# Self attention in a two-layer decoder: GpSimd rounds the fourth key tile's powers, ScalarE raises that tile once

## What is computed

```python
q, k, v = split_heads(x @ w_q), split_heads(x @ w_k), split_heads(x @ w_v)
attn = jax.nn.softmax(jnp.einsum('bnqd,bnkd->bnqk', q, k) * HEAD_DIM ** -0.5, axis=-1)
o = jnp.einsum('bnqk,bnkd->bnqd', attn, v)
y = merge_heads(o) @ w_proj + b_proj + x
y = (y - mean(y)) * rsqrt(var(y) + EPS) * ln_gamma + ln_beta
```

## Time and profile before

| | us |
|---|---|
| median of 3 runs | 2188.49 (2183.98 to 2189.59) |
| the profiled execution | 2170.81 |
| its span on the core | 2169.0 |
| self attention in it | about 52 to 1053 |
| sequence 3 in it | 430.15 to 554.74 |
| granted TensorE clock, mean | 0.887 of 2.4 GHz |

### The profile page before, as it was taken

How to read it: one execution, slowest core, us unless ns; L and a number is a source line. 1 busy time by engine, 2 the same in 40 slices (tenths; PEclk the granted TensorE clock), 3 DMA queues, 4 the chain that set the end, 5 groups by cost and what they waited for, 6 DMA issues and landing times. The chain is left out here.

```text
span 2169.0 us, 43206 instructions
## 1 busy us (share of the span) xinstructions
PE 1670.8 (77%) x13315; PEld 1065.8 (49%) x13332; DVE 1538.7 (71%) x3296; ACT 1447.3 (67%) x2314; POOL 761.0 (35%) x733
## 2 busy tenths in 40 slices
PE   3889999999999999999479887222444579987677
PEld 1455555555555555555357765122222356665323
DVE  6877777787777777777443666574788478776765
ACT  2889989889898988989334665653556334442845
POOL 0444545555454545546200000455000355553000
PEclk9999999999999999999867988655667689998799
DMA  6223222223222222222142220172010411331002
GB/s 196 54 53 67 55 65 57 67 56 67 55 65 57 66 54 55 67 55 67 32 157 78 79 75 5 60 251 88 30 58 20 135 37 26 34 39 20 1 10 69
DMA packets 173818, 139.96 MB, mean 65 GB/s; under 512 B 83794, under 2 KB 155399, under 8 KB 173366
## 3 DMA queue, kind: packets, MB, share of 16 engines
q1 hardware_dynamic: 166710, 122.78, 21.2%
q0 software_dynamic: 6912, 14.71, 3.5%
HBM read 61.92 MB, written 20.97 MB: 38 GB/s over the span
## 5 line engine op out<-in xcount | busy, mean ns | idle before, releaser
L580 ACT ACTIVATE a_p_hi<-ps,a_probs_up,a_s_scale 128x512 f16<-128x512 f32 x512 | 397.8, 777 | 70.0 <-ACTq L578 69.2
L581 ACT ACTIVATE a_probs<-ps,a_probs_up,a_s_scale 128x512 f32<-128x512 f32 x512 | 397.6, 777 | 0.0
L695 DVE TENSOR_REDUCE a_top<-ps 128x2 f32<-128x1024 f32 x256 | 313.2, 1223 | 118.6 <-DVEq L694 118.5
L927 POOL TENSOR_TENSOR a_p_lo<-a_probs,a_p_hi 128x1024 f16<-128x1024 f32 x128 | 277.4, 2167 | 244.3 <-POOLq L926 201.8
L915 POOL TENSOR_TENSOR a_ops<-a_ident_down,a_top 64x256 f16<-64x256 f32 x256 | 159.8, 624 | 288.1 <-POOLq L910 279.6
L704 DVE TENSOR_TENSOR a_p_lo<-a_probs,a_p_hi 128x1024 f16<-128x1024 f32 x128 | 183.8, 1436 | 39.2 <-DVEq L703 39.2
L441 PE MATMUL ps<-a_ops 128*128 128x512 f16 x512 | 195.1, 381 | 14.6 <-PEq L439 14.3
L460 PE MATMUL ps<-a_v_hi,a_p_hi 128*128 128x65 f16 x2048 | 202.1, 196 | 4.4 <-PEq L455 4.2
L463 PE MATMUL ps<-a_v_lo,a_p_hi 128*128 128x64 f16 x2048 | 202.1, 194 | 0.0
L464 PE MATMUL ps<-a_v_hi,a_p_lo 128*128 128x65 f16 x2048 | 202.1, 195 | 0.0
L460 PEld LDWEIGHTS ps<-a_v_hi,a_p_hi 128*128 128x128 f16 x2048 | 189.1, 98 | 25.1 <-issue 14.2
(11 more groups left out here) (497 smaller groups left out, 3702.9 us busy)
## 6 DMA issues: line engine op xcount, KB each, us to landing
a_ops<-a_qk SPq DMA_DIRECT2D x384, 128.0 KB, 2.3
f_w<-in_L_ffn_W_dram SPq DMA_DIRECT2D x16, 1024.0 KB, 7.4
a_qd<-a_qk SPq DMA_DIRECT2D x128, 64.0 KB, 2.2
g_stage<-in_L_attn_gp_w_dram SPq DMA_DIRECT2D x8, 1024.0 KB, 6.0
X<-in_x_dram SPq DMA_DIRECT2D x8, 512.0 KB, 9.6
expert_in<-f_outT SPq DMA_DIRECT2D x8, 512.0 KB
g_stage<-in_L_attn_dp_w_dram SPq DMA_DIRECT2D x8, 512.0 KB, 7.4
e_x_in<-expert_in SPq DMA_DIRECT2D x8, 512.0 KB, 4.4
```

The costliest lines, as they stand in the source:

```text
L580: nc.scalar.activation(p_hi[:, h % 2, k, :], scores, ACT.Exp, bias=probs_up[:], scale=s_scale[:])
L581: nc.scalar.activation(probs[:, h % 2, k, :], scores, ACT.Exp, bias=probs_up[:], scale=s_scale[:]).then_inc(st_taken, 1)
L695: nc.vector.tensor_reduce(top[:, c % 2, 2 * pair:2 * pair + 2], ps[:, ROW:ROW + 2, :], AX.X, ALU.max).then_inc(row_taken, 1)
L927: nc.gpsimd.tensor_tensor(p_lo[:, h % 2, 2:KT, :], probs[:, h % 2, 2:KT, :], p_hi[:, h % 2, 2:KT, :], ALU.subtract).then_inc(p_made_pool, 1)
```

## The change

`powers` leaves out the first raising for the fourth key tile (k = 3). GpSimd, when told that the fourth tile's full powers are there, rounds them itself to float16 into `p_hi`, drains, and then subtracts as before.

```diff
@@ powers(h, k), ScalarE
                     scores = ps[:, st_bank(h * KT + k), :]
-                    nc.scalar.activation(p_hi[:, h % 2, k, :], scores, ACT.Exp, bias=probs_up[:], scale=s_scale[:])
+                    if k < KT - 1:
+                        nc.scalar.activation(p_hi[:, h % 2, k, :], scores, ACT.Exp, bias=probs_up[:], scale=s_scale[:])
                     nc.scalar.activation(probs[:, h % 2, k, :], scores, ACT.Exp, bias=probs_up[:],
                                          scale=s_scale[:]).then_inc(st_taken, 1)
@@ rest(h), GpSimd
                     pool.wait_ge(probs_ready_pool, 1)
                     pool.sem_inc(probs_ready_pool, -1)
+                    nc.gpsimd.tensor_copy(p_hi[:, h % 2, KT - 1, :], probs[:, h % 2, KT - 1, :])
+                    pool.drain()
                     nc.gpsimd.tensor_tensor(p_lo[:, h % 2, 2:KT, :], probs[:, h % 2, 2:KT, :], p_hi[:, h % 2, 2:KT, :],
                                             ALU.subtract).then_inc(p_made_pool, 1)
```

## The result

| | before | after |
|---|---|---|
| median (all runs of both) | 2186.23 us (2183.52 to 2189.59, 4 runs) | 2206.77 us (2204.78 to 2215.14, 4 runs) |
| the profiled execution | 2170.81 | 2208.32 |
| its span | 2169.0 | 2206.5 |
| the attention's last value products begin at | 1052.7 | 1071.3 |

The ratio is 1.0076, with a 95% interval of 1.0042 to 1.0110: some 16.6 us more (the medians of the table lie 20.5 apart); by either the time is above the upper end of my range, 2202 us. The attention itself became 18.6 us longer. The two profiled executions differ by 37.5 us; the other 19 us lie behind the attention, in code that is the same in both. That part took 1111 to 1135 us in the profiled executions of this case, so I compare attentions and ratios, not spans.

The account below looks back on a forecast made before the run. TensorE sets the pace (busy 116.60 of 124.59 us in sequence 3), ScalarE close behind. Terms -6 - 1.8 + 0.6 + 1.8 + 11.3 = +5.9 us gave 2194.4 us; 8 in 10 range 2179 to 2202.

Parts of the forecast that it names:

- ScalarE late in heads 7 and 8: Heads 7 and 8: ScalarE, over 2 us behind, catches up with one raising less a head, ending score-bank waits: -6 us.
- head 10's L141, to head 11: Head 10: VectorE's tiny L141, shut out by GpSimd's subtraction, comes free 0.3 us earlier in six sequences: -1.8 us.
- GpSimd late at the end: Last sequence: nothing hides GpSimd's added pass and drain (0.80 us against 0.67 saved) before the last value products: +0.6 us.
- head 1, at the full clock: Head 1, sequences 2 to 7: GpSimd's subtraction, ahead of VectorE's pair, ends 0.3 us later and TensorE waits longer: +1.8 us.
- head 14, at the full clock: Head 14, sequences 1, 2, 3, 4 and 6: GpSimd's subtraction gets between VectorE's pair, 2.26 us each: +11.3 us.
- L427 is already waiting, so all of it counts: Head 14: TensorE already waits for the row maximum, so VectorE's whole 2.26 us delay was counted.
- Heads that are not named keep their times: Assumption stated for the rivals: heads without a term of their own stay as long as before.
- the forecast collision: Head 14: GpSimd's pass starts 0.08 us before VectorE's pair, and the subtraction shuts out the second of the pair.
- The pass: GpSimd's added rounding of 128x512 ahead of its subtraction: taken as 0.65 us, with the drain 0.80, range 0.76 to 1.22.
- The dear pass: Rival: GpSimd's rounding takes 1.07 us and TensorE waits for GpSimd; sum +10.6, 2199.1 us; chance 0.13.
- Who starts first: GpSimd and VectorE exclude each other on SBUF reads; in head 14 GpSimd's rounding comes 0.08 us before VectorE's pair.
- late enough to hold an L441: Sign of being wrong: a GpSimd diagonal (L915) so late that TensorE's score product L441 waits for it.

Follow-up runs that it names:

- pool_only: The kernel before with GpSimd's rounding and drain added, ScalarE still raising the fourth tile twice: ratio 1.0090 to the kernel before.
- fill_after: The changed kernel with five more unused 128x512 products where TensorE stands still in heads 1 and 14: ratio 1.0017 to the kernel before.
- act_only: The changed kernel without GpSimd's rounding and drain, the fourth tile's high half zero: ratio 1.0027 to the kernel before.
- no_read: The changed kernel with GpSimd's rounding replaced by an equally long pass that only writes zeros to an unused tile: ratio 0.9932 to the kernel before.

## Why the prediction was wrong

The whole attention, by the prediction's terms, from the lengths of the heads in both traces:

| term | predicted | measured |
|---|---|---|
| ScalarE late in heads 7 and 8 | -6 | -4.7 |
| head 10's L141, to head 11 | -1.8 | -1.6 |
| GpSimd late at the end | +0.6 | +1.9 |
| head 1, at the full clock | +1.8 | +1.4 |
| head 14, at the full clock | +11.3 | +7.1 |
| nine half-clock stretches more | none | +14.8 |
| sum | +5.9 | +18.9 |

(The measured sum is 0.3 over the 18.6 because heads that changed by under 0.15 us are left out.)

**The step that failed** is the sentence on head 14, "L427 is already waiting, so all of it counts", and the one on head 1, "The wait of TensorE in head 1 grows by that": both price a wait at its own length, and "Heads that are not named keep their times" extends that to the rivals. The sum treats the granted clock as fixed at the level that the earlier trace rows shows. It isn't: in after it fell behind eight of the ten standstills of 2.2 us or more in heads 1 and 14. In head 1 that turned 0.23 us of wait into 1.8 to 1.9 us a head in four of six sequences, and 0.5 into 2.1 in sequence 5; in head 14 of sequences 2 and 6 it added 1.6 us to 2.2. Five of the nine stretches stand in head 1, the term that I thought the most harmless, two in head 14 with the forecast collision, one in head 14 of sequence 7, and one in head 10, where the wait had grown by 0.05 us only. The number of stretches is in part luck: pool_only has waits as long in head 1 and one stretch for them. No rival held it. The trace of before had it on show: the one head 14 with the collision, in sequence 5, lies in this window of before, which I read for its timeline and not for its clock:

```profile
782.00:799.00 17.00, 14.85 (x146) 9.68 (x144) 14.07 (x16) 12.65 (x20) 8.03 (x8) 0.90 0.25 55
```

Had I carried over that head as a whole (12.17 us against 8.73, so 3.4 us) and not its VectorE chain (2.26), five sequences would have given 17 us.

Point by point:
- **The pass.** 0.61 us measured, 0.65 taken, from the line through GpSimd's small one-input rows. The dear pass was no danger. The Trainium skill's 769 ns ("GPSIMD Engine Reference", section "Elementwise — side-by-side cycle accounting") is a quarter above what this chip shows for 512 elements. Two of the prediction's sums on a longer pass are too low by its own working: 0.12 us more would have added 1.3 us (five heads 14 and six heads 1), not 0.6 to 1, and at 1.07 us head 1 would have cost 0.7 us, not 0.4.
- **Who starts first.** The order of pass, pair and subtraction in head 14 was right to 0.01 us in sequences 1, 2 and 6 (0.09 ahead; predicted 0.08), and so was the 0.06 us by which the subtraction comes ahead of the pair's second (0.66 and 0.72 behind the pair's start). In 3 and 4 it was wrong by 0.25 and 0.23 us: in 3 VectorE was early, since L705 had not been held by the diagonals, in 4 ScalarE was late. A margin of 0.08 us was too thin for one answer in five sequences; a share of each would have been the better term.
- **Head 1.** Pass and subtraction ahead of the pair (the subtraction by 0.13 us), 2.67 us for it: the mechanism as described, 0.23 a head instead of 0.3.
- **ScalarE's relief.** The bank waits of heads 7 and 8 are gone (no idle time at L441 there), head 7 takes 7.05 us instead of 7.6. In head 8 the row maxima come 0.8 us late instead of 0.5, which eats a quarter.
- **The end.** I took one head's 0.13 us and a little more. In sequence 7 GpSimd's lateness counts twice. The first time it is not the low halves but a diagonal, which the prediction had as a sign of being wrong ("late enough to hold an L441"). GpSimd's diagonals of head 11, before and after, and the L441 with which head 12 begins, after:

```profile
1020.96 0.61 POOL L915 TENSOR_TENSOR a_ops<-a_ident_down,a_top 64x256 f16<-64x256 f32 x1 [0.31 <-POOLq L910]
```

```profile
1036.76 1.45 POOL L916 TENSOR_TENSOR a_ops<-a_ident_down,a_top 64x256 f16<-64x256 f32 x1 [0.31 <-POOLq L911]
1038.51 0.38 PE L441 MATMUL ps<-a_ops 128*128 128x512 f16 x1 [1.78 <-PEq L439]
```

  GpSimd comes 0.8 us later in its head, falls behind VectorE's L705, which reads from 1036.51 on, and is shut out; heads 11 and 12 together are 1.2 us longer. The second time it is the value products of head 14, which start 0.75 us later in their head. Together 1.9 us, three times the term. Head 14 is 2.4 us longer, though, and the rest is a stretch once more. From the first value product to the next head, before and after:

```profile
1039.56:1042.81 3.25, 3.25 (x56) 2.96 (x57) 1.74 (x3) 3.05 (x5) 0.00 (x0) 1.00 0.01 3
```

```profile
1056.46:1061.35 4.89, 4.89 (x56) 4.27 (x57) 1.77 (x3) 1.72 (x3) 2.73 (x2) 0.65 0.01 2
```

  The same 56 matmuls take 1.64 us longer at a granted clock of 0.65. No wait of 2 us stands in front of this stretch, but three of about 1 us within 5 us (0.88, 0.86 and 1.19).

Of the two errors that matter, the clock (+14.8) and the mild collisions (-4.2), the second hid a part of the first. That was luck.

## What to carry to other kernels
Before pricing an edit by a wait, look what the granted clock does behind waits of that kind in the same trace; a standstill that grows by a quarter of a microsecond can cost eight times that (1.88 us for 0.23 in head 1 of sequence 3), and one that is filled with useless products can be cheaper than one left empty. Work that moves onto GpSimd has to be placed against VectorE's two-input instructions to a tenth of a microsecond, and it is safer to move the VectorE instruction away from what TensorE waits for than to hope for the order; that took the changed kernel from 0.8% slower than the kernel before to 0.5% faster, 0.2% of which is the move alone. When a pattern is to repeat, carry over the whole length of the stretch in which the trace already has it, not the one chain in it that explains it.

## What the runs showed of the hardware
- **The clock.** TensorE, busy 92% of the attention of after (581 of 630 us from 430 on), was granted 1.2 GHz for some 3.5 us behind most standstills of 2.2 us or more in heads 1 and 14 (start to start, less the products' own time), at about 1.65 us each; behind the six of 1.93 us in head 1 of the kernel before never. But 2.5 us in head 14 of sequence 1 and 2.16 in head 1 of sequence 4 had none behind them, six of 2.3 to 2.5 us in head 1 of pool_only had one in all, and 2.1 to 2.3 in head 10 of after had one in a single sequence, so the length of the last wait alone doesn't decide; what else does was not tried. The Trainium skill, "TensorE: Matmul & The Clock Gate", section "Part 1: The HAM clock gate (the "warmup" mystery)", says that this clock goes by how busy TensorE has recently been; fill_after agrees, where the same collisions with the standstills filled left no stretch.
- **Two instructions of VectorE in a row are no unit.** A read of GpSimd that waits when the first ends gets in before the second: subtractions 0.15 us (act_only, sequence 4: 2.75 us for the pair), 0.29 us (before, sequence 5: 2.75) and 0.66 us (after, sequence 2, where the first had itself been held: 3.07) behind the pair's start, and the rounding 0.16 us behind it (1.24, the second 0.83 us instead of 0.48). A subtraction 0.59 us behind an unhindered pair, when the second has begun, lets both through (0.88).
- **A GpSimd pass that only writes** (415.41 in no_read) runs beside VectorE's two-input instruction with neither longer (0.61 and 0.88 us).
